# Reordering the key, value and output projections of a cross-attention and feed-forward kernel

## The chip, the cores and the metric

One Trainium2 chip, one core. The metric is the device time of one execution in microseconds (us), the median of several runs.

## The reference

Eight batches of 256 tokens with 512 features pass through a cross-attention and then a feed-forward block, each with a residual.

```python
# per batch; x [256, 512], ctx [256, 512]; 8 groups of 4 heads, head width 16
xn = layernorm(x)
q = xn @ Wq.T + bq                     # 32 heads
k = ctx @ Wk.T + bk                    # 8 key groups
v = ctx @ Wv.T + bv
w = softmax(mask(q @ k.T / 4))         # [32, 256, 256]
x1 = x + (w @ v) @ Wo.T + bo
hn = act_quant(rms_norm(layernorm(x1)))
h = gelu(silu(hn @ weight_quant(W1).T + b1))      # [256, 2048]
h = layer_norm(h) * ln_g + ln_b
out = x1 + act_quant(rms_norm(h)) @ weight_quant(W2).T + b2
```

## The kernel before

The batches go through a software pipeline. `over_batches` calls the `body` of every engine for n = -1 to 9 with four batch numbers: c = n is the batch whose second scores, exponentials and weighted sums are made, a = n+1 the one whose key, value and first scores are made, f = n-1 the one in layer one of the feed-forward part, t = n-2 the one in layer two. w = a+1 is the batch whose x is turned and whose queries are projected. "Iteration 3" below is that with c = 3, so a = 4, w = 5, f = 2, t = 1. Each engine works its own queue strictly in the order in which `body` writes it; semaphores (`wait_ge`) tie the queues together. There is no planner.

What TensorE (PE) does in iterations 2 to 6, in this order:

- head: `turn_x(w)`, `project_out(f, 0)`, `turn_max(c)`, `project_q(w)`, `project_out(f, 1)`, `project_k(a)`, `project_v(a)`;
- second scores: for g = 0 to 8, `scores_2(c, 2g)`, `scores_2(c, 2g+1)`, then `values(c, 2g-2)`, `values(c, 2g-1)`; `turn_xq(f)` after g = 5, `turn_hq(t, 0)` and `(t, 1)` after g = 7, `(t, 2)` and `(t, 3)` after g = 8;
- first scores: 16 pieces of `scores_1(a, n)`, each followed by a piece of `layer_1(f)` or `layer_2(t)`.

In iteration 6 there is no w, in iteration 7 (`last_body_of`) no a, and iterations 8 and 9 are the feed-forward tail of batches 7 and 6.

The PSUM tile FF has two banks. `project_q` writes r = 0, 1 into the first and r = 2, 3 into the second; ScalarE (ACT, L1111) makes a bf16 part of each r and VectorE (DVE, L1389, `query_rests`) the rest of each. The semaphores q_made and r1q_made count these, four for a batch. `project_k` (L731) then writes 256 columns of the first bank, `project_v` (L741) 256 columns of the second. `keys` (L1119) and `values_in` (L1128) read them on ScalarE; the latter fills `vaug`, which `values` (L813) reads and waits for through v_placed. `scores_2` (L797) alternates between the PSUM tiles S0 and S1 and waits from n = 2 on until `exps` (L1136) has read scores n-2. `exps` number n writes slot n mod 4 of PT, which `values` n reads.

ScalarE's queue in the head: `turned_x(w)` (L1103), `squares(t, 0)` (L1194), `queries(w, 0)`, `queries(w, 1)`, `squares(t, 1)`, an exponential of one column (L1264) before which the table of exponentials is loaded, `keys(a)`, `values_in(a)`, then the 16 exponentials with the copies `values_out` (L1149) among them. The iteration ahead of it ended with silu (L1170), gelu (L1177) and Square (L1185).

VectorE's queue in the second-scores stage holds the key's rests, then for the feed-forward of f: `centre_2` (L1469, L1472), `scale_1` (L1479 to L1484), `quantise_1` (L1490), `bias_scale` (L1496 to L1513, whose last signal is b_9), `scale_2(t)` (L1627, two instructions on 2048 columns), `turn_1(f)` (L1519, L1522), and where there is a w below 7 `norm_1(w+1)`; then `turn_2(t)` (L1635). PE's `turn_xq` needs the quantised rows of L1490 (L849 transposes them) and then b_9 (L855); `turn_hq(t, 0)` (L905) needs `turn_1(f)` and `scale_2(t)`.

GpSimd (POOL) does tensor_tensor work through one helper, L510. In its queue `residual_2(f)` adds b2 to x1 (128x1024, L510 x<-x,b_bc), followed by `residual(c)` (L510 xb_sb<-xb_sb,bo_bc) and `divide(c)`. In iterations 1 to 4 they stand behind `norm_1_apply(w+1)` (L527); from iteration 5 on there is no such batch. In iteration 7 `residual(c)` comes first.

In iteration 7 PE works `turn_hq_last`, `layer_1(f, 4)`, `layer_1(f, 5)`, `project_out(7, 0)`, `project_out(7, 1)`, `layer_1(f, 6)`. The next VectorE work of `last_hidden` is `residual_1(7, 0)` (L1451), `spread_last`, `gain(t, 0)` (L1565), `residual_1(7, 1)` and `norm_2`, in this order.

Of the kernel before, what the change touches and what calls it, by code (L numbers as in the profile page):

```python
# [6 lines left out]
ACT = mybir.ActivationFunctionType  # L7
# [8 lines left out]
B, T, D = 8, 256, 512  # L16
# [37 lines left out]
def build(nc, x, ctxT, mask_q, mask_k, mask_row0, pad, wq, wkv, wo, bq, bk, bv, bo,  # L54
          w1, b1, ln_g, ln_b, w2, b2, out):
    with ExitStack() as ctx:
# [88 lines left out]
        def x1_of(b):  # L145
            return xb_sb[:] if b == B - 1 else x1[:, b % 2, :, :]
# [62 lines left out]
        def pair_of(a):  # L209
            return S1[:, :, :].rearrange("p r t -> p (r t)") if a < 2 else FFw  # L210
# [57 lines left out]
        def next_front(a):  # L268
            return a + 1 if a is not None and a + 1 < B else None
# [218 lines left out]
        def _(pool):  # L488
# [20 lines left out]
            def tt(out_, in0, in1, op, signal):  # L509
                pool.tensor_tensor(out_, in0, in1, op).then_inc(S[signal], 1)  # L510
# [43 lines left out]
            def residual_2(f):  # L554

                if at_start(f):
                    pool.wait_ge(S["w_two"], 48)
                pool.wait_ge(S["hn_made"], 2 * f + 2)
                tt(x1_of(f), x1_of(f), b2_bc[:].unsqueeze(1).broadcast_to([P, TT, D]),
                   ALU.add, "x1b_made")  # L560

# [92 lines left out]
        def _(pe):  # L654
# [60 lines left out]
            def project_k(a):  # L715
                if at_start(a):
                    pe.wait_ge(S["w_kv"], 16)
                pe.wait_ge(S["ctx_in"], 16 * a + 16)
                if a == 1:
                    pe.wait_ge(S["k_made"], 1)  # L720
                    pe.wait_ge(S["r1k_made"], 1)
                    pe.wait_ge(S["v_placed"], 1)
                elif 1 < a < B - 1:
                    pe.wait_ge(S["q_made"], 4 * a + 8)
                    pe.wait_ge(S["r1q_made"], 4 * a + 8)
                elif a > 1:
                    pe.wait_ge(S["silu_made"], 8 * (a - 2))
                    pe.wait_ge(S["out_made"], 2 * (a - 3))
                to = pair_of(a)
                for k in range(KD):  # L730
                    last = pe.matmul(to[:, 0:T], wkv_sb[:, k, 0:P], ctx_sb[:, k, :],  # L731
                                     start=(k == 0), stop=(k == KD - 1))
                last.then_inc(S["k_ps"], 1)

            def project_v(a):
                if a == 1:
                    pe.wait_ge(S["v_placed"], 1)
                to = pair_of(a)
                for t in range(TT):
                    for k in range(KD):  # L740
                        last = pe.matmul(to[:, 512 + t * P:512 + (t + 1) * P],  # L741
                                         ctx_sb[:, k, t * P:(t + 1) * P], wkv_sb[:, k, P:2 * P],
                                         start=(k == 0), stop=(k == KD - 1))
                last.then_inc(S["kv_ps"], 1)
# [203 lines left out]
            def body_of(c, a, f, t, masked):  # L948
                w = next_front(a) if c > 1 else None
                if w is not None:  # L950
                    turn_x(w)
                if f is not None and not at_start(f):
                    project_out(f, 0, c)
                turn_max(c)
                if at_start(f):
                    project_out(f, 0, c)
                if at_start(c):
                    weight_sum(0)
                    project_q(2, (2, 3))
                if w is not None:  # L960
                    project_q(w)
                if f is not None:
                    project_out(f, 1, c)
                if a is not None and a > 1:
                    project_k(a)
                    project_v(a)
                for g in range(G + 1):
                    if c is not None and g < G:
                        scores_2(c, 2 * g, masked)
                        scores_2(c, 2 * g + 1, masked)  # L970
                    if c is not None and g > 0:
                        values(c, 2 * g - 2)
                        values(c, 2 * g - 1)
                    if at_start(f) and g == 2:
                        weight_sum(1)
                    if f is not None and g == 5:
                        turn_xq(f, a)
                    if t is not None and g == 7:
                        turn_hq(t, 0, f)
                        turn_hq(t, 1, f)  # L980
                if t is not None:
                    turn_hq(t, 2, f)
                    turn_hq(t, 3, f)

                for n in range(16):
                    if a is not None:
                        scores_1(a, n, masked)
                    if at_start(c):
                        if 1 <= n <= 4:
                            output_bias(n - 1)  # L990
                        if n == 8:
                            turn_x(3)
                        if n in (10, 12, 14, 15):
                            project_q(3, ((10, 12, 14, 15).index(n),))
                    if f is not None and n < 8:
                        layer_1(f, n, t)
                    if t is not None and n >= 8:
                        layer_2(t, n - 8, f)

            def last_body_of(c, f, t, masked):  # L1000

                if c is not None:
                    project_out(f, 0, c)
                    turn_max(c)
                    project_out(f, 1, c)
                    run_on(S1w[:, 0:512], 7)
                    pe.wait_ge(S["out_made"], 2 * t)
                    for g in range(G + 1):
                        if g < G:
                            scores_2(c, 2 * g, masked)  # L1010
                            scores_2(c, 2 * g + 1, masked)
                        if g < 2:
                            run_on(FF[:, 1, :], 3)
                        if g > 0:
                            values(c, 2 * g - 2)
                            values(c, 2 * g - 1)
                        if g == 5:
                            turn_xq(f, None)
                        if g == 7:
                            layer_1(f, 0, None)  # L1020
                    for n in range(1, 4):
                        layer_1(f, n, None)
                    for n in range(4):
                        turn_hq_last(t, n)
                    layer_1(f, 4, None)
                    layer_1(f, 5, None)
                    project_out(c, 0, None)
                    project_out(c, 1, None)
                    layer_1(f, 6, None)
                    layer_1(f, 7, None)  # L1030
                    layer_2_last(t, 0)
                elif f is not None:
                    turn_xq_last(f)
                    for n in range(8):
                        layer_1(f, n, None)
                    layer_2_last(t - 1, 1)
                    for n in range(4):
                        turn_hq_last(t, n)
                    for tok in range(TT):
                        layer_2_last(t, tok)  # L1040
                else:
                    run_on(PVw[:, 0:512], 24)
                    turn_hq_last(t, 0)
                    turn_hq_last(t, 1)
                    run_on(PVw[:, 0:512], 8)
                    layer_2_last(t, 0)
                    run_on(PVw[:, 0:512], 6)
                    turn_hq_last(t, 2)
                    turn_hq_last(t, 3)
                    layer_2_last(t, 1)  # L1050
# [38 lines left out]
        def _(act):  # L1089
# [143 lines left out]
            def body(c, a, f, t):  # L1233
# [3 lines left out]
                if at_start(a):  # L1237
# [12 lines left out]
                    weight_abs_sum(0, (3,))  # L1250
                    return
                w = next_front(a) if c != 1 else None
                if w is not None and c > 0:
                    turned_x(w)
                if t is not None:
# [3 lines left out]
                    queries(w, 1)  # L1259
                if t is not None and a is not None:  # L1260
                    squares(t, 1)
                if c is not None:

                    act.activation(table_call[:, 1:2], table_call[:, 0:1], ACT.Exp)  # L1264
                if a is not None and a > 1:
                    keys(a)
                    values_in(a)
                if c is not None:
                    for n in range(16):
                        exps(c, n)  # L1270
                        if n in (5, 9, 13):
                            values_out(c, (n - 5) // 4)
                    values_out(c, 3)
# [621 lines left out]
```

## Time and profile before

| what | us |
|---|---|
| median of 3 runs | 583.21 |
| lowest, highest | 582.84, 586.53 |
| the profiled execution, its whole time | 581.34 |
| its span, first to last instruction | 579.3 |
| an iteration of the middle (3: PE's first transpose at 220.91, the next one's at 283.49) | 62.58 |
| PE busy in the span | 520.6 (90%) |
| DVE busy in the span | 491.1 (85%) |
| ACT busy in the span | 351.4 (61%) |
| POOL busy in the span | 139.9 (24%) |

All rows below come from the one profiled execution. Its whole time is its span and 2.04 us around it. Times of rows are microseconds from the span's start.

### The profile page before, as it was taken

How to read it: one execution, taken by the hardware profiler on the slowest of the kernel's cores; microseconds unless marked ns; L12 is line 12 of the kernel's file. 1: busy time of each engine (PE TensorE's matmuls, PEld its weight loads, DVE VectorE, ACT ScalarE, POOL GpSimd, SP SyncE). 2: the span in 40 equal slices, each digit the busy share in tenths (PEclk: the TensorE clock that was granted, in tenths of full speed). 3: DMA queues.
4: the chain of work that ended last, by engine and by line, in shares of the span. 5: the costliest groups of instructions: out<-in, count | busy, mean ns of one | idle time of the engine just before them, and what ended most of it. 6: DMA issues, size and time to landing. Idle time of an engine off the chain costs nothing.

```text
span 579.3 us, 9027 instructions
## 1 busy us (share of the span) xinstructions
PE 520.6 (90%) x3425; PEld 285.6 (49%) x3425; DVE 491.1 (85%) x730; ACT 351.4 (61%) x424; POOL 139.9 (24%) x106
## 2 busy tenths in 40 slices
PE   4978788999899999899999999999949999798796
PEld 3856335544564557445663566445514553243343
DVE  4689929789989788988999789978896889959996
ACT  2235470687848764785659573866368576876931
POOL 5103034003410621025200611211122105133130
PEclk9986899999899999999999999999969999988999
DMA  6888595887126712463137502571115411110002
GB/s 200 277 209 317 174 279 156 335 304 170 37 66 197 163 43 79 160 179 86 72 117 183 117 16 98 161 170 40 43 39 140 101 40 42 27 30 1 36 2 75
DMA packets 32994, 72.17 MB, mean 125 GB/s; under 512 B 7167, under 2 KB 14529, under 8 KB 29950
## 3 DMA queue, kind: packets, MB, share of 16 engines
q1 hardware_dynamic: 31286, 67.13, 39.6%
q0 software_dynamic: 576, 4.19, 1.8%
q8 instruction: 29, 0.48, 0.4%
q10 hardware_dynamic: 1088, 0.24, 0.2%
q14 instruction: 15, 0.12, 0.1%
HBM read 46.50 MB, written 20.61 MB: 116 GB/s over the span
## 4 chain that ended last, share of the span: by engine, by line
PE 54%; DVE 20%; issue 8%; DMA 7%; ACT 7%; POOL 2%; SPq 2%; ACTq 0%; DVEq 0%
PE FF L891 8%; PE FF L943 6%; DVE negm L1416 5%; PE S L773 5%; PE PV L813 5%; ACT PT L1136 5%; PE PV L830 4%; PE S L797 4%; PE FF L710 3%; DMA num<-o_raw 2%; PE PV L773 2%; PE FF L893 2%; DVE work L1565 2%; POOL st L510 2%; PE FF L905 2%
## 5 line engine op out<-in xcount | busy, mean ns | idle before, releaser
L1136 ACT ACTIVATE PT<-S 128x1024 f32<-128x1024 f32 x128 | 123.4, 1032 | 24.0 <-PE S L797 23.6
L1416 DVE TENSOR_REDUCE negm<-S 128x4 f32<-128x1024 f32 x88 | 105.6, 1215 | 17.9 <-PE S L773 16.5
L797 PE MATMUL S<-Q,K 100*128 100x512 bf16 x256 | 73.7, 393 | 18.6 <-ACT PT L1136 14.9
L891 PE MATMUL FF<-w1t,xqT 128*128 128x512 bf16 x256 | 68.4, 390 | 5.0 <-ACT wq_sb L1170 3.4
L813 PE MATMUL PV<-PT,vaug 128*32 128x256 f32 x1024 | 70.5, 394 | 0.6 <-ACT PT L1136 0.6
L773 PE MATMUL S<-K,Q 97*128 97x256 bf16 x352 | 55.5, 284 | 5.4 <-DVE negm L1416 3.5
L830 PE MATMUL PV<-wo_sb,num 128*128 128x512 f32 x128 | 59.1, 608 | 0.0
L1170 ACT ACTIVATE work<-FF,s 128x512 f32<-128x512 f32 x48 | 33.0, 687 | 36.3 <-PE FF L893 36.3
L1416 DVE TENSOR_REDUCE negm<-PV 128x4 f32<-128x1024 f32 x40 | 48.8, 1220 | 5.6 <-PE PV L773 5.2
L710 PE MATMUL FF<-xnT,wq_sb 128*128 128x256 f32 x224 | 50.6, 381 | 0.2 <-ACT xnT L1103 0.2
L1194 ACT ACTIVATE work<-work 128x2048 bf16<-128x2048 f32 x12 | 22.9, 1911 | 45.2 <-DVE work L1571 45.0
L797 PEld LDWEIGHTS S<-Q,K 100*128 100x128 bf16 x256 | 18.1, 98 | 64.7 <-ACT PT L1136 49.6
L510 POOL TENSOR_TENSOR st<-st,const 128x1 f32<-128x1 f32 (+1 forms) x26 | 27.1, 1042 | 92.7 <-DVE st L1561 44.5
L773 PEld LDWEIGHTS S<-K,Q 97*128 97x128 bf16 x352 | 33.8, 100 | 28.4 <-DVE negm L1416 7.1
L813 PEld LDWEIGHTS PV<-PT,vaug 128*32 128x32 f32 x1024 | 27.0, 111 | 39.4 <-issue 24.8
L710 PEld LDWEIGHTS FF<-xnT,wq_sb 128*128 128x128 f32 x224 | 41.7, 190 | 5.8 <-ACT xnT L1103 0.5
L510 POOL TENSOR_TENSOR s<-s,const 128x2 f32<-128x2 f32 (+1 forms) x17 | 13.5, 803 | 127.7 <-DVE s L1463 101.3
L943 PE MATMUL FF<-w2t,work 128*128 128x512 bf16 x160 | 41.1, 378 | 0.0
L891 PEld LDWEIGHTS FF<-w1t,xqT 128*128 128x128 bf16 x256 | 24.7, 99 | 29.0 <-issue 5.9
L830 PEld LDWEIGHTS PV<-wo_sb,num 128*128 128x128 f32 x128 | 24.5, 196 | 25.7 <-issue 25.0
L510 POOL TENSOR_TENSOR num<-num,rec 128x1024 f32<-128x1024 f32 (+1 forms) x8 | 18.8, 2351 | 63.8 <-DMA rec<-rec_d 60.4
L510 POOL TENSOR_TENSOR rs<-rs,const 128x2 f32<-128x2 f32 x8 | 5.6, 696 | 108.9 <-DVE rs L1376 108.8
(231 smaller groups left out, 905.2 us busy)
## 6 DMA issues: line engine op xcount, KB each, us to landing
Q<-q_d SPq DMA_DIRECT2D x15, 768.0 KB
q_d<-part SPq DMA_DIRECT2D x8, 768.0 KB, 3.6
x_sb<-in_x SPq DMA_DIRECT2D x8, 512.0 KB, 4.1
ctx_sb<-in_ctxT SPq DMA_DIRECT2D x8, 512.0 KB, 4.6
work<-in_w SPq DMA_DIRECT2D x4, 1024.0 KB, 13.2
q_d<-part SPq DMA_DIRECT2D x8, 512.0 KB, 3.3
xb_sb<-in_x SPq DMA_DIRECT2D x8, 512.0 KB, 4.3
work<-in_w POOLq DMA_DIRECT2D x4, 1024.0 KB, 8.9
```

The lines of the kernel that those rows point to most:

```text
L510: pool.tensor_tensor(out_, in0, in1, op).then_inc(S[signal], 1)
L710: last = pe.matmul(to[:, r, :], wq_sb[:, k, r * P:(r + 1) * P], xnT[:, k, :], start=(k == 0), stop=(k == KD - 1))
L773: last = pe.matmul(to[:, r, :], Q[0:ROWS_1, g, r, t * P:(t + 1) * P], K[0:ROWS_1, g, :], start=not masked, stop=True)
L797: last = pe.matmul(where, K[0:ROWS_2, g, kt * P:(kt + 1) * P], Q[0:ROWS_2, g, 2 * pair:2 * pair + 2, :], start=not masked, stop=True)
L813: last = pe.matmul(PV[32 * r:32 * r + 32, g % 4, :], vaug[:, c % 2, kt, g, :], PT[:, n % PT_SLOTS, r, :], start=(kt == 0), stop=(kt == TT ...
L830: last = pe.matmul(PVw[:, 512 * t:512 * (t + 1)], num[:, g, t * P:(t + 1) * P], wo_sb[:, g, :], start=(g == 0), stop=(g == R - 1))
L891: pe.matmul(FF[:, n % 2, :], xqT[:, k, t * P:(t + 1) * P], w1t[:, k, cols], start=(k == 0), stop=False)
L943: last = pe.matmul(FF[:, tok, :], hqT[:, k, tok * P:(tok + 1) * P], w2t[:, k, :], start=(k == 0), stop=(k == KI - 1))
L1136: act.activation(PT[:, n % PT_SLOTS, :, :], ST[n % 2][:], ACT.Exp, scale=0.25).then_inc(S["pt_made"], 1)
L1170: act.activation(h_of(f, t)[:, c * 512:(c + 1) * 512], FF[:, n % 2, :], ACT.Silu, scale=s2[:, 7, t:t + 1]).then_inc(S["silu_made"], 1)
L1194: act.activation(squared, h_of(t, tok), ACT.Square, accum_out=s3[:, 2, tok:tok + 1]).then_inc(S["sq_made"], 1)
L1416: dve.tensor_reduce(negm[:, t, R * g:R * g + R], RING_1[n % 3][:], AX.X, ALU.max, negate=True).then_inc(S["max_made"], 1)
```

## The change

Five edits. K's projection in iterations 3 to 5 waits for two rests of Q in place of four, and V's projection takes the wait for the other two. V's projection moves behind the first two second scores, and its copy on ScalarE behind the exponential of n = 2. The one-column exponential that loads the table moves to the head of ScalarE's iteration. GpSimd's addition of b2 also waits for b_9. In iteration 7 `project_out(7, 0)` moves ahead of `layer_1(f, 4)` and `layer_1(f, 5)`.

```diff
@@ gpsimd, residual_2
                 pool.wait_ge(S["hn_made"], 2 * f + 2)
+                pool.wait_ge(S["b_9"], f + 1)
                 tt(x1_of(f), x1_of(f), b2_bc[:].unsqueeze(1).broadcast_to([P, TT, D]),
@@ tensor, project_k
-                elif 1 < a < B - 1:
-                    pe.wait_ge(S["q_made"], 4 * a + 8)
-                    pe.wait_ge(S["r1q_made"], 4 * a + 8)
+                elif a == 2:
+                    pe.wait_ge(S["q_made"], 16)
+                    pe.wait_ge(S["r1q_made"], 16)
+                elif 2 < a < B - 1:
+                    pe.wait_ge(S["q_made"], 4 * a + 6)
+                    pe.wait_ge(S["r1q_made"], 4 * a + 6)
@@ tensor, project_v
                 if a == 1:
                     pe.wait_ge(S["v_placed"], 1)
+                if 2 < a < B - 1:
+                    pe.wait_ge(S["q_made"], 4 * a + 8)
+                    pe.wait_ge(S["r1q_made"], 4 * a + 8)
@@ tensor, body_of
                     project_k(a)
-                    project_v(a)
                 for g in range(G + 1):
                     if c is not None and g < G:
                         scores_2(c, 2 * g, masked)
                         scores_2(c, 2 * g + 1, masked)
+                    if g == 0 and a is not None and a > 1:
+                        project_v(a)
@@ tensor, last_body_of
                         turn_hq_last(t, n)
+                    project_out(c, 0, None)
                     layer_1(f, 4, None)
                     layer_1(f, 5, None)
-                    project_out(c, 0, None)
                     project_out(c, 1, None)
@@ scalar, body
                 w = next_front(a) if c != 1 else None
+                if c is not None:
+                    act.activation(table_call[:, 1:2], table_call[:, 0:1], ACT.Exp)
                 if w is not None and c > 0:
                     turned_x(w)
...
-                if c is not None:
-
-                    act.activation(table_call[:, 1:2], table_call[:, 0:1], ACT.Exp)
                 if a is not None and a > 1:
                     keys(a)
-                    values_in(a)
                 if c is not None:
                     for n in range(16):
                         exps(c, n)
+                        if n == 2 and a is not None and a > 1:
+                            values_in(a)
```

## Rows read from the trace of the kernel before

**Rows 1.** The page: chain that ended last, share of the span by engine.

```profile
PE 54%; DVE 20%; issue 8%; DMA 7%; ACT 7%; POOL 2%; SPq 2%; ACTq 0%; DVEq 0%
```

**Rows 2.** Timeline, head of iteration 3: start, duration, engine, line, count, [idle before <-releaser].

```profile
221.99 1.01 ACT L1103 COPY xnT<-S 128x1024 f32<-128x1024 f32 x1 [1.21 <-PE S L696]
...
225.33 7.13 PE L710 MATMUL FF<-xnT,wq_sb 128*128 128x256 f32 x32
...
235.09 1.65 DVE L1389 SCALAR_TENSOR_TENSOR rest<-FF,bq_sb,part 128x256 f32<-128x256 f32 x4
...
236.89 1.97 PE L731 MATMUL FF<-ctx_sb,wkv_sb 128*128 128x256 f32 x8 [1.00 <-DVE rest L1389]
...
237.23 1.28 ACT L1264 ACT_TABLE_LOAD   x1
...
238.69 1.95 PE L741 MATMUL FF<-wkv_sb,ctx_sb 128*128 128x128 f32 x16
238.89 0.47 ACT L1119 ACTIVATE part<-FF,bk_sb 128x256 bf16<-128x256 f32 x1 [0.17 <-PE FF L731]
...
240.48 1.03 PE L797 MATMUL S<-Q,K 100*128 100x512 bf16 x4
...
241.11 3.77 ACT L1136 ACTIVATE PT<-S 128x1024 f32<-128x1024 f32 x4
...
243.64 1.07 PE L813 MATMUL PV<-PT,vaug 128*32 128x256 f32 x16
```

**Rows 3.** Timeline, iteration 3, where the other engines meet the second-scores stage.

```profile
251.96 0.17 DVE L1513 TENSOR_TENSOR inv<-s,inv 128x2 bf16<-128x2 f32 x1
...
253.57 0.28 PE L855 MATMUL FF<-identb,inv 128*128 128x128 bf16 x2
...
258.50 1.29 DVE L1635 TENSOR_SCALAR work<-FF 128x1024 bf16<-128x1024 int16 x2 [1.51 <-PE FF L905]
```

**Rows 4.** Source view of L731 (K): what ended PE's idle time, us, times.

```profile
  DVE rest L1389: 3.0, 3
```

**Rows 5.** Source view of L1128 (V's copy): ns min/median/max, first and last start.

```profile
L1128 ACT COPY vaug<-FF x6: 361/372/372, 118.6 to 427.7; 128x256 f32<-128x256 f32 x6
```

**Rows 6.** Timeline, head of iteration 6.

```profile
425.99 1.28 ACT L1264 ACT_TABLE_LOAD   x1
...
428.00 1.95 ACT L1136 ACTIVATE PT<-S 128x1024 f32<-128x1024 f32 x2
...
429.09 1.95 PE L797 MATMUL S<-Q,K 100*128 100x512 bf16 x4 [7.40 <-ACT PT L1136]
...
430.97 1.51 PE L813 MATMUL PV<-PT,vaug 128*32 128x256 f32 x12
```

**Rows 7.** Windows: length, busy PE, PEld, DVE, ACT, POOL, PEclk, DMA share, GB/s.

```profile
424.90:435.10 10.20, 6.01 (x31) 1.51 (x35) 9.84 (x21) 8.15 (x12) 3.69 (x3) 0.50 0.27 78
```

**Rows 8.** Timeline, iteration 5, VectorE and GpSimd around b_9, and the first transposes of `turn_hq`.

```profile
376.87 2.39 POOL L510 TENSOR_TENSOR xb_sb<-xb_sb,bo_bc 128x1024 f32<-128x1024 f32 x1 [1.82 <-DMA xb_sb<-in_x]
...
377.08 2.20 DVE L1509 TENSOR_TENSOR s<-s,inv 128x2 f32<-128x2 f32 x1
...
382.00 0.69 DVE L1519 TENSOR_SCALAR xqT<-FF 128x1024 bf16<-128x1024 int16 x1
...
384.05 1.07 PE L905 MATMUL FF<-identb,work 128*128 128x128 bf16 x16
```

**Rows 9.** Source view of L1484: ns min/median/max, first and last start.

```profile
L1484 DVE SCALAR_TENSOR_TENSOR s<-s x8: 160/163/536, 121.5 to 527.2; 128x2 f32<-128x2 f32 x8
```

**Rows 10.** Timeline, iteration 7, GpSimd's addition against VectorE.

```profile
486.96 4.17 POOL L510 TENSOR_TENSOR xb_sb<-xb_sb,bo_bc 128x1024 f32<-128x1024 f32 x1
...
488.82 2.99 DVE L1469 TENSOR_SCALAR rec<-x,mv 128x512 f32<-128x512 f32 x2
```

**Rows 11.** Timeline, end of iteration 7, output projection and residual of batch 7.

```profile
515.42 6.60 PE L830 MATMUL PV<-wo_sb,num 128*128 128x512 f32 x15
...
522.13 0.69 DVE L1451 TENSOR_TENSOR xb_sb<-PV,xb_sb 128x512 f32<-128x512 f32 x1 [0.42 <-PE PV L830]
```

## The prediction

> **What bounds the kernel now.** I read the page's busy shares first, then the chain that ended last: PE is busy for 90% of the span, VectorE for 85%, and the chain lies on PE for 54% and on VectorE for 20% [rows 1]. Neither share says what an edit is worth, so I went through the timeline of one middle iteration and asked at each stage which wait ends last. Three stages repeat. In the **head**, VectorE's queue is the bound: it works without a gap up to the rests of Q, and PE, done with the output projection, stands idle 1.00 us until the fourth rest is made [rows 2]. In the **second scores** the exponentials on ScalarE follow each other without a gap, so this stage ends as much earlier as its loop is started earlier. In the **first scores** PE is the bound. The VectorE side is close behind: b_9 is made at 252.13 and PE comes for it at 253.57, and VectorE waits 1.51 us before it turns the second layer's input [rows 3]. A gain in the head of up to some 1.4 us therefore goes right through, and a larger one would be cut.
>
> **K earlier.** The four rests start at 235.09 and take 1.65, so 0.41 each; the second is done at 235.92, the fourth at 236.74. K started 0.15 behind the fourth, and would start 0.15 behind the second, at 236.05: 0.84 us earlier. This happened in three iterations, each with 1.00 of idle time [rows 4]; those are 3, 4 and 5. In iterations 1, 2 and 6 K follows PE's own work, and this edit gives nothing.
>
> **V behind the first two scores.** In iteration 3 today: V 238.69, scores 240.48 (1.79 later), first exponential 241.11 (0.63 behind the scores), first `values` 243.64, which is 4.95 behind V [rows 2]. After the change: scores 0 at 236.05 + 1.80 = 237.85; the key's copy comes 2.00 behind K's start and takes 0.47, so exponential 0 starts at 238.5, 2.6 us earlier than now. That is not the gain, though. V starts behind two score groups (four matmuls, some 0.9 us) at 238.73, which leaves it where it was; scores 2 start 1.79 later, at 240.52, exponential 2 at 241.15, ending at 242.1 (0.94 each from the four in 3.77); V's copy takes 0.37 [rows 5] and ends at 242.5, and `values` 0 starts there. So `values` gains 243.64 - 242.5 = **1.1 us**, of which K gives 0.84 and the reordering 0.25. Scores 4 stand behind `values` on PE, so everything later moves by the same 1.1. What hides the rest: the two early exponentials have nowhere to go, since V, scores 2 and V's copy are a chain behind them. Iterations 3 and 4: **2.2 us**. Iterations 1 and 2, without K's part: 0.2 each, **0.4 us**. Queued behind the new wait of V are scores 2, but the fourth rest is done at 236.74, 2 us before V comes, so the wait costs nothing. The load of the next context waits for V's end, 240.7 before and after.
>
> **The table at the head.** The load takes 1.28 us and its one-column instruction some 0.2. At the head it stands before the copy of the turned x, which waits until 221.99 while ScalarE is idle 1.21; the load can begin at 220.78, so the copy starts at 222.3 and ends at 223.3, and `project_q` comes at 225.33 [rows 2]. Two microseconds of cover: cost nothing. Where it stood it was hidden by K in iterations 2 to 5. In iteration 6 it was not: there Square ends at 425.97, then come load, key's copy, V's copy, and the first exponential at 428.00, with PE idle 7.40 us [rows 6]. Without the load, the key's copy runs 425.99 to 426.45, exponential 0 starts at 426.4, scores 2 at 427.5 (1.09 behind, as now). PE is at its lower level there, granted clock 0.50, that is 1.2 GHz [rows 7], so two score groups take 1.95; exponential 2 starts 1.07 behind scores 2, takes 0.97, V's copy 0.36, `values` 0 comes at 429.9 in place of 430.97: **1.05 us**.
>
> The Trainium skill ("ScalarE: Activation LUTs", What ACT_TABLE_LOAD costs) adds a drain of 1.38 us to the same 1.28 us for each switch. Row 425.99 and the exponential at 428.00 leave no room for it, so I don't count it; by the page iteration 6 would give up to 1.4 us more, and the head would still be covered.
>
> **b2's addition behind b_9.** In iterations 1 to 4 GpSimd comes to it long after b_9 (261.97 against 252.13 in 3), no effect. In iteration 5 it ran beside L1472 and L1484, which took 0.54 in place of its median 0.163 [rows 9], and left `residual(c)` to run at 376.87, beside L1509: 2.20 in place of 0.16 [rows 8]. Both engines stop each other. With the wait, both blows before b_9 go: 0.37 + 2.04 = 2.4 us earlier, at 377.3, and PE's wait for it (0.86) is gone. The addition then falls on the two instructions of `scale_2(t)`, which stand right behind b_9. VectorE is first by 0.1; GpSimd gets its turn between the two, as `residual(c)` did in iteration 7, where it was held 1.9 us and then held L1469 (2.99 in place of 0.88) [rows 10]. That gives 2.35 back: `turn_1` stays at 382.0, done at 382.9. `turn_hq` needs it, ran at 384.05 and would without this be due 1.1 + 1.0 earlier; it starts at 382.9. Iteration 5 gains **1.15 us**, not 2.1. In iteration 6 the same shift is hidden: PE comes late there. In iteration 7 only L1484's 0.37 counts; b_9 is on the path (PE waited 0.53 for it), and what follows it on VectorE for 2.3 us is a reduction, beside which such an addition ran free of cost in iteration 5 (L1472, 1.22): **0.35 us**.
>
> **Wo ahead of two pieces of layer one.** PE works without a gap from the transposes on, and the two halves of the projection end at 522.0, wherever the two pieces (1.08 each) stand. `residual_1(7, 0)` comes 2.16 earlier, and `gain` behind it, but the next, `residual_1(7, 1)`, waits for PE until 522.13 [rows 11], and all of `norm_2` stands behind it. No gain. It can cost: the projection now needs GpSimd's quotient, ready at 512.76, and PE comes at 512.8. Between 0 and 0.3 us; I take 0.
>
> **Sum.** 0.4 + 2.2 + 1.15 + 1.05 + 0.35 = 5.15, say 5.1 us. The profiled execution would come to 581.34 - 5.1 = 576.2. It lies 1.87 below the median, so for the median 583.21 - 5.1 = **578.1 us**.
>
> **Rivals.**
> - *More comes through* (0.22). VectorE keeps its turn for both instructions of `scale_2`, and GpSimd waits: iteration 5 gains 2.1, total 6.1, 577.1. Or PE's spell at the lower level in iteration 6 (10.2 us, PE the bound in it) ends a third earlier, since PE resumes 1.6 us sooner: up to 1.7 more. Centre 576.4. For: L1484's kind of stall shows GpSimd first only where it came first. Against: rows 10. The Trainium skill ("SBUF — State Buffer", SBUF: two separate sides) says that whichever starts first holds the shared port pair for the whole instruction; it leaves open who has it between two of VectorE's.
> - *Less comes through* (0.20). Either K's early start is lost, because PE is held by something that the four rests hide (its weight load shows 1.80 us of issue before K): 0.84 three times off, 580.6. Or GpSimd keeps the pair for both additions: `turn_1` of iteration 5 ends 2.35 later, at 385.3, behind the 384.05 of now, and 1.15 of gain turns into 1.25 of loss: 580.5.
> - *Slower* (0.05). TensorE's clock. Each microsecond at the lower level where PE is the bound costs half of one. The spell of rows 7 is the model; if the moved holes in the heads of iterations 2 and 6 and in the tail lengthened such spells by over 10.2 us in all, the 5.1 would be gone. With four spells each longer by a third of that one (3.4): +6.8 - 5.1, 584.9. Against: no head gets a longer hole than it had; 7.40 becomes about 6.
> - *It does nothing* (0.03): the stages are bound elsewhere, 583.
>
> **How the numbers follow.** Forecast 0.50, around it some 1 us for the runs' own scatter. One per cent, about what a measurement can tell from no change, is 5.8 us: below 577.4 is faster. That is the first rival and a third of the forecast's own scatter: 0.38. Slower by over 1% would be above 589.0: 0.03. The rest, 0.59, is within. The range 575.6 to 581.6 takes in the first two rivals and leaves out the last two and their neighbours.
>
> **What the profile will show.** K at once behind the output projection, idle under 0.2 in iterations 3 to 5; first exponentials 2.6 us earlier with a hole of some 0.7 before exponential 2; `values` 1.1 earlier; iterations 3 and 4 at 61.5 us in place of 62.6. In iteration 5 L1509 at 0.16 and one L1627 at 3.6. In iteration 7 `residual_1(7, 0)` early, `residual_1(7, 1)` still behind L830. I would be wrong if the exponentials' loop were not the bound of its stage (then the gain is under 1.1 although `values` starts early), or if a second table load appeared in the head, because Square or Identity is not served by the table of exponentials; in iteration 7 Square runs behind exponentials with no load between.

## The result and the profile after

The changed kernel takes **575.75 us** (median of 4 runs, 573.66 to 576.68) where the kernel before takes 583.9 us in the same sitting. The ratio is 0.9849, with a 95% interval of 0.9805 to 0.9893: 1.5% faster. The forecast was 578.1, with 0.38 on more than 1% faster and 0.59 on within 1%. The direction holds. The median lies 0.15 inside the stated range of 575.6 to 581.6, by luck: the forecast started from 583.21, and the measured ratio of that is 574.4, below the range. The likeliest class does not hold either, because the gain was sized too small.

The profiled execution took 576.15, its span is 573.9 (before 579.3). The page's share of the chain has moved from ScalarE to VectorE; compare [rows 1]:

```profile
PE 52%; DVE 25%; issue 8%; DMA 6%; ACT 3%; POOL 2%; SPq 1%; ACTq 0%; DVEq 0%
```

Line numbers have shifted: L731 is L735, L741 L748, L797 L804, L813 L820, L855 L862, L905 L912, L1119 L1127, L1128 L1136, L1136 L1144, L1170 L1178, and VectorE's lines are up by 8. First the timeline after, head and second scores of iteration 3, against [rows 2, 3]. The iteration starts 1.04 later than before (its silu load at 199.48 against 198.44), so subtract 1.04 to compare.

```profile
221.83 1.28 ACT L1262 ACT_TABLE_LOAD   x1
223.12 0.20 ACT L1262 ACTIVATE table_call<-table_call 128x1 f32<-128x1 f32 x1
223.23 0.99 ACT L1111 COPY xnT<-S 128x1024 f32<-128x1024 f32 x1
...
236.12 1.65 DVE L1397 SCALAR_TENSOR_TENSOR rest<-FF,bq_sb,part 128x256 f32<-128x256 f32 x4
237.14 1.96 PE L735 MATMUL FF<-ctx_sb,wkv_sb 128*128 128x256 f32 x8 [0.21 <-DVE rest L1397]
238.94 1.03 PE L804 MATMUL S<-Q,K 100*128 100x512 bf16 x4
239.57 1.94 ACT L1144 ACTIVATE PT<-S 128x1024 f32<-128x1024 f32 x2
239.80 1.95 PE L748 MATMUL FF<-wkv_sb,ctx_sb 128*128 128x128 f32 x16
241.59 1.03 PE L804 MATMUL S<-Q,K 100*128 100x512 bf16 x4
242.22 1.02 ACT L1144 ACTIVATE PT<-S 128x1024 f32<-128x1024 f32 x1 [0.71 <-PE S L804]
242.70 1.07 PE L820 MATMUL PV<-PT,vaug 128*32 128x256 f32 x16
243.15 0.37 ACT L1136 COPY vaug<-FF 128x256 f32<-128x256 f32 x1
243.40 2.89 ACT L1144 ACTIVATE PT<-S 128x1024 f32<-128x1024 f32 x3
...
252.98 0.17 DVE L1521 TENSOR_TENSOR inv<-s,inv 128x2 bf16<-128x2 f32 x1
253.20 0.28 PE L862 MATMUL FF<-identb,inv 128*128 128x128 bf16 x2 [0.40 <-DVE inv L1521]
253.96 1.03 ACT L1144 ACTIVATE PT<-S 128x1024 f32<-128x1024 f32 x1 [1.05 <-PE S L804]
...
260.66 1.28 ACT L1178 ACT_TABLE_LOAD   x1 [0.45 <-PE FF L912]
```

The table load, K and the first exponential are where the forecast put them: the load covered, the wait of K 1.00 down to 0.21, exponential 0 at 239.57 - 1.04 = 238.53 against 238.5. Then comes what I had not foreseen: `values` 0 starts at 242.70, **before** V's copy at 243.15. It is 242.70 - 1.04 = 241.66 in the clock of before, 1.98 earlier than 243.64, not 1.1. By b_9 PE has run so far ahead that it waits 0.40 for VectorE where it had 1.44 to spare, and the iteration keeps 1.40 of the 1.98.

The lengths of the iterations, from one load of silu's table (L1170, now L1178) to the next, show all of it; 260.66 - 199.48 = 61.18 is iteration 3. The first column is iteration 1, from `turn_max(1)` on; "exps 7" runs from iteration 6's load to iteration 7's; b2 stands for b2's wait. The other rows are the experiments below.

| kernel | 1 | 2 | 3 | 4 | 5 | 6 | exps 7 |
|---|---|---|---|---|---|---|---|
| before | 30.13 | 60.54 | 62.58 | 62.58 | 63.62 | 62.75 | 55.48 |
| changed | 29.22 | 58.35 | 61.18 | 61.24 | 62.28 | 60.63 | 55.09 |
| changed, second profile | 29.19 | 58.04 | 61.20 | 61.25 | 62.28 | 60.21 | 55.09 |
| forecast of it | 29.9 | 60.3 | 61.5 | 61.5 | 62.5 | 61.7 | 55.1 |
| V only | 29.18 | 58.28 | 61.40 | 61.40 | 64.97 | 61.89 | 55.47 |
| K only | 30.13 | 60.62 | 61.80 | 61.79 | 63.78 | 62.21 | 55.48 |
| table only | 30.14 | 59.61 | 62.58 | 62.57 | 63.60 | 60.31 | 55.46 |
| changed, V's copy later | 29.07 | 58.47 | 61.20 | 61.25 | 62.28 | 60.90 | 55.11 |
| changed, b2 free | 29.19 | 58.13 | 61.21 | 61.25 | 65.05 | 60.76 | 55.48 |
| changed, table back | 29.18 | 58.51 | 61.20 | 61.25 | 62.28 | 61.80 | 55.10 |
| changed, factors later | 29.18 | 58.30 | 60.86 | 60.77 | 65.53 | 60.95 | 55.10 |
| changed, b2 later | 29.17 | 58.17 | 61.21 | 61.25 | 61.21 | 60.98 | 55.11 |
| changed, both | 29.18 | 58.48 | 60.85 | 60.76 | 60.53 | 60.40 | 55.10 |

Changed against before: 0.91 + 2.19 + 1.40 + 1.34 + 1.34 + 2.12 + 0.39 = 9.7 us from iteration 1 on. The spans differ by 5.4 only, because in this execution the part ahead of `turn_max(1)` took 4.14 more (111.91 against 107.77). That part is not the change: a second profile of the same changed kernel has it at 107.64.

### The profile page after: what moved, and what is told of

It is laid out like the page before. It is cut to its first block, busy times and chain, and to the rows that moved or that the text cites. A ratio compares the mean times of both kernels' runs of the same rounds, so it can differ in the third digit from the quotient of the medians.

```text
span 573.9 us, 9038 instructions
## 1 busy us (share of the span) xinstructions
PE 523.6 (91%) x3425; PEld 288.8 (50%) x3425; DVE 490.3 (85%) x730; ACT 350.9 (61%) x424; POOL 143.6 (25%) x106
## 4 chain that ended last, share of the span: by engine, by line
PE 52%; DVE 25%; issue 8%; DMA 6%; ACT 3%; POOL 2%; SPq 1%; ACTq 0%; DVEq 0%
PE FF L898 8%; PE FF L950 6%; PE S L780 6%; DVE negm L1424 6%; PE PV L837 4%; PE PV L820 4%; PE S L804 4%; PE FF L711 3%; ACT PT L1144 2%; PE PV L780 2%; DVE s L1584 2%; PE FF L900 2%; DVE work L1573 2%; POOL st L510 2%; PE FF L912 2%
## 5 line engine op out<-in xcount | busy, mean ns | idle before, releaser
L1144 ACT ACTIVATE PT<-S 128x1024 f32<-128x1024 f32 x128 | 124.6, 1032 | 25.8 <-PE S L804 25.4
L804 PE MATMUL S<-Q,K 100*128 100x512 bf16 x256 | 74.1, 398 | 11.7 <-ACT PT L1144 5.9
L820 PE MATMUL PV<-PT,vaug 128*32 128x256 f32 x1024 | 70.3, 393 | 0.8 <-ACT PT L1144 0.6
L780 PE MATMUL S<-K,Q 97*128 97x256 bf16 x352 | 57.0, 290 | 5.7 <-DVE negm L1424 3.0
L1178 ACT ACTIVATE work<-FF,s 128x512 f32<-128x512 f32 x48 | 33.0, 687 | 36.3 <-PE FF L900 36.3
L804 PEld LDWEIGHTS S<-Q,K 100*128 100x128 bf16 x256 | 18.6, 99 | 56.4 <-ACT PT L1144 37.0
L820 PEld LDWEIGHTS PV<-PT,vaug 128*32 128x32 f32 x1024 | 27.1, 110 | 39.4 <-issue 25.7
```

Of the source, the lines that this page charges most:

```text
L780: last = pe.matmul(to[:, r, :], Q[0:ROWS_1, g, r, t * P:(t + 1) * P], K[0:ROWS_1, g, :], start=not masked, stop=True)
L804: last = pe.matmul(where, K[0:ROWS_2, g, kt * P:(kt + 1) * P], Q[0:ROWS_2, g, 2 * pair:2 * pair + 2, :], start=not masked, stop=True)
L820: last = pe.matmul(PV[32 * r:32 * r + 32, g % 4, :], vaug[:, c % 2, kt, g, :], PT[:, n % PT_SLOTS, r, :], start=(kt == 0), stop=(kt == TT ...
L1144: act.activation(PT[:, n % PT_SLOTS, :, :], ST[n % 2][:], ACT.Exp, scale=0.25).then_inc(S["pt_made"], 1)
L1178: act.activation(h_of(f, t)[:, c * 512:(c + 1) * 512], FF[:, n % 2, :], ACT.Silu, scale=s2[:, 7, t:t + 1]).then_inc(S["silu_made"], 1)
```

## Experiments

Each is timed against runs of the kernel before that were interleaved with its own on the same chip. The first four take the change apart.

**V only.** The kernel before, with V and its copy moved, nothing else.

```diff
                     project_k(a)
-                    project_v(a)
...
+                    if g == 0 and a is not None and a > 1:
+                        project_v(a)
...
-                    values_in(a)
...
+                        if n == 2 and a is not None and a > 1:
+                            values_in(a)
```

Expected: 

> The kernel before, with only V behind the first two score groups and its copy behind exponential 2. K still waits for all four rests. Theory 1: V(a) serves the next batch, so `values(c, 0)` never waits for its copy; moving it takes 1.2 us per iteration out of the way in iterations 1 to 5 (iteration 3: `values` 0 starts 1.15 to 1.3 earlier against the head, b_9's slack of 1.44 lets all of it through). Iteration 6 gains 0 to 1. Total 6 to 7 us, ratio near 0.989. Theory 2, my prediction: the copy gates `values` 0, 0.25 per iteration, total 1.2 us, ratio 0.998.

Measured: 578.0 us, ratio 0.9913 (0.9881 to 0.9945). Iterations 3 and 4 gain 1.18 each, iteration 1 0.95, iteration 6 0.86: theory 1. But iteration 5 **loses** 1.35, so the total is 5 and not 6 to 7. Timeline of this kernel, iteration 5, against [rows 8], then busy times and granted clock of a window behind it, with the same stretch of `K only` (the next experiment) under it:

```profile
373.85 2.43 POOL L510 TENSOR_TENSOR xb_sb<-xb_sb,bo_bc 128x1024 f32<-128x1024 f32 x1 [1.24 <-DMA xb_sb<-in_x]
373.98 2.33 DVE L1498 TENSOR_SCALAR s<-s,wz 128x2 f32<-128x2 f32 x1
...
377.38 0.40 PE L855 MATMUL FF<-identb,inv 128*128 128x128 bf16 x2 [2.09 <-DVE inv L1515]
377.57 1.91 PE L797 MATMUL S<-Q,K 100*128 100x512 bf16 x4
379.41 1.66 PE L813 MATMUL PV<-PT,vaug 128*32 128x256 f32 x16
```

```profile
377.20:380.60 3.40, 3.22 (x18) 1.24 (x22) 3.30 (x5) 1.94 (x2) 0.00 (x0) 0.51 0.28 63
```

```profile
380.10:383.50 3.40, 3.32 (x30) 1.16 (x34) 3.15 (x4) 2.62 (x4) 0.00 (x0) 1.00 0.35 84
```

PE comes earlier, but a two-element instruction of VectorE (2.33, 0.22 where it is undisturbed) is still held by GpSimd's addition, so PE's wait for b_9 grows from 0.86 to 2.09. That alone would only eat the gain: the transposes behind the wait start 56.21 after the iteration's silu load, before 56.16. The loss comes behind it. The granted clock drops to 0.51, TensorE's lower level of 1.2 GHz, and the next scores take 1.91 and `values` 1.66 where they took 1.03 and 1.07 before. From these transposes to the first of `turn_hq` it is 5.59 (377.38 to 382.97) against 4.29 before (379.76 to 384.05): 1.3 of the 1.35.

**K only.** K waits for two rests; V, right behind it, for all four.

```diff
-                elif 1 < a < B - 1:
-                    pe.wait_ge(S["q_made"], 4 * a + 8)
-                    pe.wait_ge(S["r1q_made"], 4 * a + 8)
...
+                elif 2 < a < B - 1:
+                    pe.wait_ge(S["q_made"], 4 * a + 6)
+                    pe.wait_ge(S["r1q_made"], 4 * a + 6)
...
+                if 2 < a < B - 1:
+                    pe.wait_ge(S["q_made"], 4 * a + 8)
+                    pe.wait_ge(S["r1q_made"], 4 * a + 8)
```

Expected: 

> The kernel before, with only K waiting for two rests; V stands right behind K. Both theories: K starts 0.84 us earlier in iterations 3, 4 and 5, all of it goes through, 2.5 us in all, ratio 0.9957. A third theory, that K's early start is lost (PE held by something that the rests hide): 0, ratio 1.000.

Measured: 581.69 us, ratio 0.9999 (0.9974 to 1.0024), which alone would speak for "lost". The iterations say more: 3 and 4 gain 0.78 and 0.79 (forecast 0.84), 5 loses 0.16. There b_9 holds PE for 1.80, again because a two-element instruction of VectorE took 2.43 beside GpSimd's addition; the granted clock stays at 1.00. So 1.4 of the expected 2.5 arrives, less than these runs can tell from nothing.

**Table only.** The load at the head in the kernel before.

```diff
+                if c is not None:
+                    act.activation(table_call[:, 1:2], table_call[:, 0:1], ACT.Exp)
                 if w is not None and c > 0:
...
-                    act.activation(table_call[:, 1:2], table_call[:, 0:1], ACT.Exp)
                 if a is not None and a > 1:
```

Expected: 

> The kernel before, with only the table of the exponentials loaded at the head. Both theories: nothing in iterations 1 to 5, in iteration 6 the 1.28 us of the load, cut to about 1.0 to 1.3 by PE at its lower level; ratio 0.998. If the spell at the lower level ends earlier too, up to 1.7 more, ratio 0.995.

Measured: 581.72 us, ratio 0.9981 (0.9957 to 1.0004). Iterations 3 to 5 are unchanged within 0.02. Iteration 6 gains 2.44, the load and 1.2 more. The granted clock over the window that matches [rows 7] is 0.71 in place of 0.50, so the spell at the lower clock is shorter. Not all of that is the edit's: `K only`, whose edit doesn't reach iteration 6, has 0.67 there and is 0.54 shorter. Iteration 2 shows 0.93 that neither theory has; see the last section.

**V's copy later.** The changed kernel with `values_in(a)` behind exponential 4 in place of 2. If the copy gates `values`, this costs two exponentials an iteration.

```diff
-                        if n == 2 and a is not None and a > 1:
+                        if n == 4 and a is not None and a > 1:
                             values_in(a)
```

Expected: 

> The changed kernel, with V's copy behind exponential 4 in place of exponential 2. Theory 1: the copy gates nothing in the second scores, so the first `values` start where they do in the changed kernel and the total stays within 0.5 us of it (ratio to before 0.985). Theory 2: `values` 0 waits for the copy, two exponentials of 0.94 us later in each of six iterations, 8 to 11 us slower than the changed kernel, ratio to before near 1.00.

Measured: 576.59 us, ratio 0.9886 (0.9852 to 0.9920); every iteration from 2 to 5 within 0.12 of the changed kernel. Theory 2 wanted 8 to 11 us. In the timeline `values` 0 starts 2.56 ahead of the copy:

```profile
241.22 1.07 PE L820 MATMUL PV<-PT,vaug 128*32 128x256 f32 x16
...
243.78 0.37 ACT L1136 COPY vaug<-FF 128x256 f32<-128x256 f32 x1
```

The next four look at b2's wait and at what binds the changed kernel now.

**b2 free.** The changed kernel without `pool.wait_ge(S["b_9"], f + 1)`.

Expected: 

> The changed kernel without b2's wait for b_9. Theory 1: the wait is what lets iteration 5 profit. Without it GpSimd's two additions strike b_4 again, at about 2.3 us, PE waits some 2.0 us for b_9, and iteration 5 takes some 65 us (the kernel before with V's move alone took 64.97) in place of 62.28; iteration 7 loses up to 0.4; total 2.5 to 3.5 us slower than the changed kernel, ratio to before near 0.990. Theory 2, by my sum: iteration 5 gives back no more than the 1.15 that I gave to it and the turned wait, total 1.2 to 1.5, ratio 0.987.

Measured: 578.33 us, ratio 0.9914 (0.9889 to 0.9940). Iteration 5 gives back 2.77 and iteration 7 0.39, together 3.2: theory 1 by its size. Its timeline, iteration 5:

```profile
372.89 2.48 POOL L510 TENSOR_TENSOR xb_sb<-xb_sb,bo_bc 128x1024 f32<-128x1024 f32 x1 [1.17 <-DMA xb_sb<-in_x]
373.09 2.31 DVE L1503 TENSOR_SCALAR s<-s,wz 128x2 f32<-128x2 f32 x1
...
376.48 0.28 PE L861 MATMUL FF<-identb,inv 128*128 128x128 bf16 x1 [2.62 <-DVE inv L1520]
```

The changed kernel has the wait, and there, in the same place:

```profile
375.49 4.59 DVE L1635 TENSOR_SCALAR work<-work,s 128x2048 f32<-128x2048 f32 x2
375.63 0.28 PE L862 MATMUL FF<-identb,inv 128*128 128x128 bf16 x2 [0.41 <-DVE inv L1521]
375.72 3.27 POOL L510 TENSOR_TENSOR x<-x,b_bc 128x1024 f32<-128x1024 f32 x1 [7.64 <-DVE inv L1521]
378.95 3.34 POOL L510 TENSOR_TENSOR xb_sb<-xb_sb,bo_bc 128x1024 f32<-128x1024 f32 x1
380.00 0.68 DVE L1527 TENSOR_SCALAR xqT<-FF 128x1024 bf16<-128x1024 int16 x1
381.02 1.05 PE L912 MATMUL FF<-identb,work 128*128 128x128 bf16 x16 [1.03 <-DVE inv6T L1530]
```

The two additions and the two instructions of `scale_2` take turns: VectorE's pair takes 4.59 in place of 2.48, and PE waits 1.03 for the end of it.

The 2.77 can be split by these rows. Measured from the silu load, PE goes on behind b_9 at 56.21 without the wait and at 53.73 with it, 2.48 later; the 1.03 falls away; and some 1.3 is the clock again, 0.52 over 376.4 to 379.8. 2.48 - 1.03 + 1.3 = 2.75.

**Factors later.** VectorE's chain to b_9 shortened by what is not part of it.

```diff
-                if t is not None:
-                    factor_2(t)
                 if f is not None:
                     quantise_1(f)
                     bias_scale(f)
+                if t is not None:
+                    factor_2(t)
```

Expected: 

> The changed kernel with VectorE's `factor_2` (five small instructions, 0.65 us) behind `bias_scale` in place of ahead of `quantise_1`. Theory 1: VectorE's chain to b_9 cuts the gain of iterations 3, 4 and 5 at 1.4; with b_9 0.65 earlier PE's wait for it (0.40) goes, and each of the three gains 0.4 to 0.6: 1.2 to 1.8 us less than the changed kernel. Rival: something else of the stage is as late (ScalarE's row of exponentials, or VectorE's work after b_9, whose sum is unchanged), and the total stays.

Measured: 578.88 us, ratio 0.9944 (0.9923 to 0.9964), slower than the changed kernel. Iterations 3 and 4 gain 0.32 and 0.47, so b_9 was the bound there, and PE's wait of 0.40 is what the edit gives. Iteration 5 loses 3.25 (the last row is from PE's own timeline):

```profile
372.08 2.37 POOL L510 TENSOR_TENSOR x<-x,b_bc 128x1024 f32<-128x1024 f32 x1 [7.12 <-DVE inv L1521]
372.30 2.17 DVE L1600 TENSOR_SCALAR z<-s,wz 128x2 f32<-128x2 f32 x1
374.40 2.36 POOL L510 TENSOR_TENSOR xb_sb<-xb_sb,bo_bc 128x1024 f32<-128x1024 f32 x1
374.57 4.47 DVE L1635 TENSOR_SCALAR work<-work,s 128x2048 f32<-128x2048 f32 x2
...
379.99 1.86 PE L912 MATMUL FF<-identb,work 128*128 128x128 bf16 x16 [3.64 <-DVE inv6T L1530]
```

b_9 now releases the addition into `factor_2`: 2.17 for 0.21. The second addition starts just ahead of `scale_2`, whose pair takes 4.47. The transposes start 1.95 later than in the changed kernel, 61.07 after the silu load in place of 59.12. The other 1.3 is the clock: 0.51 over 379.5 to 382.9, and the sixteen transposes take 1.86 in place of 1.05. I had not looked at what the signal that I moved sets off.

**b2 later.** The addition waits for both instructions of `scale_2(t)` as well, but not in iterations 7 and 8.

```diff
                 pool.wait_ge(S["b_9"], f + 1)
+                if t is not None:
+                    pool.wait_ge(S["hs_made"], 2 * t + 2)
...
-                    residual_2(f)
+                    residual_2(f, t)
```

Expected: 

> The changed kernel with b2's addition held until both instructions of `scale_2` of the other batch are done. Theory 1: those two are then 2.48 us long in iteration 5 in place of 4.59, `turn_1` is 2.1 earlier, PE's wait of 1.03 goes: 1.0 to 1.2 us less than the changed kernel, all in iteration 5. Rival: the two additions of GpSimd then fall on `turn_1` or on the turns behind it and hold one of them by some 2 us: 0 to 1.2 us more.

Measured: 575.82 us, ratio 0.9867 (0.9833 to 0.9902). Iteration 5 at 61.21, 1.07 less, iterations 3 and 4 unchanged: theory 1. The whole times don't tell this kernel from the changed one. The additions run beside `turn_1` and the turns behind it, which keep their 0.68 and 1.29.

**Both edits.** Expected: 

> The changed kernel with both of these edits. If both theories hold they add up: 2.2 to 3.0 us less than the changed kernel, ratio to before near 0.981. If the two reliefs have one bound in common in iteration 5, 0.4 less than the sum.

Measured: 574.12 us, ratio 0.9855 (0.9819 to 0.9891). Iteration 5 is at 60.53: with the addition out of the way the earlier b_9 pays there too. The iterations give the expected 2.6, the whole time does not: its ratio is no better than the changed kernel's, and the expected 0.981 lies below its interval.

The last four stand side by side: the changed kernel, both edits, and two parts of the change undone.

**The changed kernel again.** Expected: 

> The changed kernel itself, on the same chip as the three that follow, as their measure: ratio to before 0.985 to 0.989. Iterations 2 to 6 within 0.1 to 0.3 us of the profile after (58.35, 61.18, 61.24, 62.28, 60.63).

Measured: 575.03 us, ratio 0.9853 (0.9822 to 0.9883); iterations 3 to 5 at 61.20, 61.25, 62.28.

**Both again.** Expected: 

> The changed kernel with `factor_2` behind `bias_scale` and b2's addition behind `scale_2`, beside the changed kernel on one chip: iterations 3 and 4 at 60.8, 5 at 60.5, together 2.5 us less than the changed kernel, ratio between the two 0.995 to 0.996. Rival: the time saved in the middle is given back in the end by a lower granted clock, and the two agree within 0.5 us.

Measured: 571.9 us, ratio 0.9795 (0.9760 to 0.9830): 3.1 us below the changed kernel beside it. The intervals still overlap by a little (0.9822 to 0.9830), but iterations 3 to 5 repeat the earlier profile within 0.01 and are 2.6 us shorter than the changed kernel's. It is the fastest version found. Its timeline, iteration 5:

```profile
372.38 0.29 PE L864 MATMUL FF<-identb,inv 128*128 128x128 bf16 x2
373.00 2.48 DVE L1637 TENSOR_SCALAR work<-work,s 128x2048 f32<-128x2048 f32 x2
375.39 0.68 DVE L1529 TENSOR_SCALAR xqT<-FF 128x1024 bf16<-128x1024 int16 x1
375.65 2.37 POOL L510 TENSOR_TENSOR x<-x,b_bc 128x1024 f32<-128x1024 f32 x1 [10.30 <-DVE work L1637]
376.67 1.07 PE L914 MATMUL FF<-identb,work 128*128 128x128 bf16 x16
```

From 367 to 386 no row has a wait of PE left on VectorE, and of the VectorE instructions shown none is longer than its own time.

**Table back.** The changed kernel with the load behind the squares again. Expected: 

> The changed kernel with the table of the exponentials loaded behind the squares again. Theory 1: of iteration 6's gain of 2.1 us the load is 1.3 to 2.4 (the kernel before with the load's move alone took 60.31 for it in place of 62.75), V's move 0.9: iteration 6 at 61.9 to 62.3 here, iterations 3 to 5 unchanged, 1.3 to 1.7 us slower than the changed kernel in all. Iteration 2, which was 0.93 shorter with the load's move alone, tells whether that was the move (59.2 here) or where a spell at the lower clock fell (58.3). Rival, by my sum: iteration 6 gives back 1.05.

Measured: 578.63 us, ratio 0.9893 (0.9852 to 0.9934). Iteration 6 at 61.80, iteration 2 at 58.51. The nine profiles of kernels with V moved and the load at the head have 60.21 to 60.98 for iteration 6, 60.66 in the mean: the load is worth 1.1 there, with 0.4 of scatter. Iteration 2 doesn't move, so its 0.93 in "table only" is not the load's.

**Wo back.** The last projection behind the two pieces of layer one again. Expected: 

> The changed kernel with the last projection behind the two pieces of layer one again. Both theories: within 0.3 us of the changed kernel, `residual_1(7, 1)` where it was, because it waits for the end of the projection either way.

Measured: 574.83 us, ratio 0.9845 (0.9819 to 0.9870), the same as the changed kernel beside it. From iteration 7's silu load to `residual_1(7, 1)` it is 16.61 us here (499.22 to 515.83) and 16.76 with the swap (499.90 to 516.66).

## Why the prediction was right in direction and too small

**The step that failed** is one sentence: "V's copy takes 0.37 [rows 5] and ends at 242.5, and `values` 0 starts there". The copy fills `vaug` for batch a; `values(c)` of the same stage reads batch c = a - 1, whose copy ran an iteration ago, and its wait is for v_placed at c + 1. Before, the copy stood ahead of the first exponential, where either reading fits the times; only the index in the wait tells them apart. Placing the copy two exponentials later changed no iteration. So "V, scores 2 and V's copy are a chain behind them" was wrong by its last link, and the reordering's term of **0.25 is 1.18** (V only, iterations 3 and 4). The mechanism: before, PE ran V first and then stood waiting for exponentials 0 and 1 before scores 2 and 3, for 0.68 and 0.31, in these rows of the kernel before:

```profile
242.19 0.61 PE L797 MATMUL S<-Q,K 100*128 100x512 bf16 x2 [0.68 <-ACT PT L1136]
243.10 0.60 PE L797 MATMUL S<-Q,K 100*128 100x512 bf16 x2 [0.31 <-ACT PT L1136]
```

Now V's 1.95 fills that wait; 0.71 of it is left as a hole of ScalarE, and 1.95 - 0.71 = 1.24 is close to what is measured.

**Iterations 1 and 2**, forecast 0.2 each: 0.91 and 2.19. In 1 it is the reordering (V only: 0.95). In 2 it is some 1.2 of that and 1.0 that goes with where a spell at the lower clock fell (last section).

**K**, 0.84: right as a mechanism, 0.78 in the clear. With the reordering's 1.18 it makes 1.96, and `values` 0 does come 1.98 earlier. **The cut at "some 1.4"** was right too: 1.40 and 1.34 got through, PE then waits 0.40 for b_9. In the prediction that cap had nothing to cut.

**Iteration 5**, 1.15: measured 1.34. L1509 (now L1517) is at 0.16 and the addition and `scale_2` block each other as forecast. But the wait was credited with little of it, and that split was wrong: without the wait iteration 5 takes 2.77 more. The prediction priced a late b_9 by PE's wait alone; V only, b2 free and factors later each show some 1.3 on top, at a granted clock of 0.51 to 0.52 behind a wait of 2.09, 2.62 and 3.64. The *Slower* rival named the clock, but not for this place. A part's worth depends on the others. The rival in which VectorE keeps its turn didn't come.

**Iteration 6**, 1.05: measured 2.12. The load is 1.1, as forecast. V only is 0.86 shorter there, which I had left out, but only some 0.3 of it can be V's, by the same wrong link: K only is 0.54 shorter with no edit that reaches the iteration. The other 0.5 goes with the spell at the lower level, part of a rival, which is shorter in all three: over the window that matches [rows 7] the granted clock is 0.67 in V only, K only and the changed kernel, in place of 0.50. In the changed kernel PE is busy in it for 7.80 us in place of 6.01.

```profile
421.86:432.06 10.20, 7.80 (x52) 2.28 (x56) 9.81 (x23) 8.46 (x12) 1.34 (x2) 0.67 0.24 58
```

**Iteration 7**, 0.35: 0.39, and lost again when the wait is taken out. **The Wo swap**, 0: right, `residual_1(7, 0)` comes early and `residual_1(7, 1)` waits for PE as before [rows 11].

**The drain** of 1.38 us that the Trainium skill ("ScalarE: Activation LUTs", What ACT_TABLE_LOAD costs) adds to each switch is not seen: the one-column instruction starts 0.01 after the load's end (221.83 + 1.28, then 223.12). By the page the load's move would have given up to 1.4 more in iteration 6, an estimate from its 1.38; the 1.1 measured beside V's move is the load alone.

**The sum.** Terms of 5.1 became 9.7 in the profiles and some 8.5 in the medians (583.9 - 575.75 = 8.2; ratio 0.9849 of 583.21 is 8.8 less). With 1.18 for the reordering, cut at 1.4 together with K, and 0.3 for V in iteration 6 the same working gives 1.2 + 1.2 + 1.4 + 1.4 + 1.15 + 1.35 + 0.35 = 8.05. Of the 1.6 that is left to the profiles' 9.7, 1.0 and 0.5 go with the spells of iterations 2 and 6; the first was not forecast at all, the second only as part of a rival.

## What to carry to other kernels

In a software pipeline a wait must be read with its batch index: a copy that stands in a stage may serve the next one, and then it gates nothing where it stands. When a step is moved ahead or back, price it by what the bound engine does in the time: here PE filled a wait of its own with work that nobody in the stage needed. Before a signal is moved earlier, list what it releases, on other engines too: the same 0.65 us edit lost 3.25 us in one iteration or gained 0.68 there, depending on one wait of GpSimd. Look at the granted clock behind a wait that has grown: in iteration 5 the matmuls behind a wait of 2.09 to 3.64 us cost 1.3 us more.

## What the runs showed of the hardware

**GpSimd beside VectorE.** The Trainium skill ("SBUF — State Buffer", SBUF: two separate sides) says that of the instructions that use the shared port pair whoever starts first holds it for its whole instruction; the traces agree. A VectorE instruction of two elements took 2.17 to 2.43 us behind a 2.4 us addition of GpSimd. What they add: where an addition waited behind the first of two instructions of VectorE that stand back to back, GpSimd got its turn between them. In the five profiles with the changed kernel's order (both of the changed kernel, V's copy later, table back, Wo back) this happens in iterations 5 and 6, ten times in all, and the second instruction takes 3.39 to 3.41 in place of 1.28. VectorE in turn got in between two additions. The pair of 4.47 in factors later is another case: it starts inside an addition, its first instruction takes 3.28 and its second 1.27. Not every instruction is touched: the reads of PSUM that write bf16 (L1529, 0.68; L1645, 0.69 each) ran beside an addition at full speed.

**A longer wait of TensorE and a spell at the lower clock came together.** In iteration 5 PE's longest wait was 2.09 (V only), 2.62 (b2 free) and 3.64 (factors later), and behind each the granted clock was 0.51 or 0.52 over the stretch named above, at a price of some 1.3. In the other eleven profiles no wait of PE in iteration 5 was longer than 1.81 and the granted clock of the whole iteration is 1.00 in all of them. No run varied the wait by itself, so this is an agreement of fourteen profiles and not a test.

**Where a spell at the lower clock falls matters as much as its length.** Head of iteration 2, ten microseconds from 15.0 after the silu load, before and changed, busy times, then the granted clock:

```profile
152.90:162.90 10.00, 8.25 (x27) 4.57 (x27) 9.79 (x14) 7.50 (x9) 2.54 (x3) 0.66 0.17 54
```

```profile
156.13:166.13 10.00, 9.10 (x30) 4.84 (x30) 9.79 (x14) 8.99 (x11) 2.56 (x3) 0.66 0.19 54
```

The third such window is the second profile of the changed kernel:

```profile
151.83:161.83 10.00, 7.98 (x32) 4.64 (x32) 9.79 (x15) 8.99 (x11) 2.54 (x3) 0.83 0.18 54
```

The first two have a mean of 0.66, 1.2 GHz for some 7 us, but before it begins 2 us later, leaves a stretch in which PE was waiting anyway, and reaches further into `project_out` and `project_q`. K starts 36.5 after the silu load there (174.39 - 137.90) and 35.5 in the changed kernel (176.60 - 141.13). In the third, the same code with half of the spell (0.83), it starts 35.2 after: halving it gave 0.3, its place 1.0. The same code can thus get different spells. In 14 profiles K's start was 36.5 twice, in the kernel before and in K only, whose code is the same up to there, and 35.2 to 35.6 in the twelve with V or the table moved. Whether a move sets this, or chance, stays open. No run was made for it, and 1.0 us of the gain hangs on it.

**The opening scatters.** `turn_max(1)` starts at 111.91 in one execution of the changed kernel and at 107.64 in another; over all profiles it lies between 107.64 and 113.16. In the two kernels that were profiled twice (changed, and both edits) the spans differ by 4.9 and 1.7 and the openings by 4.3 and 2.0. That is reason to compare stages, not spans.
